# Graph layer with two mixtures of experts: the second mixture on rows sorted by expert

## The reference

```python
logits = tokens @ router_w.T
probs = softmax(logits)
rw, re = top_k(probs, 2)
rw = rw / maximum(rw.sum(-1), 1e-12)
combine = zeros((N, 8)).at[arange(N)[:, None], re].set(rw)
out = tokens                       # tokens = layernorm(x)
for e in range(8):
    h = gelu(tokens @ w1[e] + b1[e])
    y = h @ w2[e] + b2[e]
    out = out + combine[:, e:e + 1] * y
```

## Time and profile before

| | us |
|---|---|
| median of 3 runs | 2085.33 |
| lowest and highest | 2073.9, 2096.82 |
| profiled execution | 2092.29, its span 2090.3 |

### The profile page before, as it was taken

One profiled execution on the slowest core, in us unless ns is written; L12 is line 12 of the kernel. 1 busy time (PEld: TensorE's weight loads), 2 busy tenths in 40 slices (PEclk: granted clock), 3 DMA queues, 4 the chain that ended last, 5 costly groups with the idle time before them and its releaser, 6 DMA issues.

```text
span 2090.3 us, 22190 instructions
## 1 busy us (share of the span) xinstructions
PE 1752.5 (84%) x6787; PEld 1057.1 (51%) x6787; DVE 965.6 (46%) x2222; ACT 576.9 (28%) x1334; POOL 659.5 (32%) x650
## 2 busy tenths in 40 slices
PE   3899477999999899971287999999998999998875
PEld 1455123444544445541244666666666666666654
DVE  5432152133233333342377566566756666664221
ACT  2111002223122231310122434343333434343231
POOL 0000475475444540004246333233433323310000
PEclk9999688999999999985567899899998989999887
DMA  7233885364453542016567545354545444421000
GB/s 226 96 126 141 279 224 140 101 189 124 133 151 101 177 115 73 16 55 238 181 175 208 145 131 145 113 160 123 149 127 143 124 132 137 129 77 32 17 5 8
DMA packets 181022, 269.96 MB, mean 129 GB/s; under 512 B 24513, under 2 KB 140181, under 8 KB 178325
## 3 DMA queue, kind: packets, MB, share of 16 engines
q1 hardware_dynamic: 140693, 144.84, 22.1%
q0 software_dynamic: 40192, 123.51, 21.1%
HBM read 196.20 MB, written 72.06 MB: 128 GB/s over the span
## 4 chain that ended last, share of the span: by engine, by line
PE 38%; DVE 6%; ACT 3%; SPq 2%; issue 2%; DMA 2%; DVEq 0%
PE att_psR L2195 8%; PE att_psR L2222 7%; PE att_psG L2089 7%; PE att_psR L2171 4%; PE att_psR L2180 3%; PE att_psE L2070 2%; DMA att_eft<-in_eft 2%; PE att_psG L2088 1%; PE att_psQ L2063 1%; SPq L2267 1%; PE att_psR L2158 1%; PE att_psR L2135 1%; DVE att_stat L1853 1%; PE att_psR L2214 1%; PE att_psG L2086 1%
## 5 line engine op out<-in xcount | busy, mean ns | idle before, releaser
L1716 POOL DMA_INDIRECT att_kv<-table_kv,g_srcI x314 | 335.2, 1067 | 735.3 <-PE att_psG L2089 477.8
L1058 POOL DMA_INDIRECT ex_hg<-table_h,z_idx x314 | 309.0, 984 | 243.7 <-PE ex_psG L1346 162.4
L2195 PE MATMUL att_psR<-att_t,g_mw 128*128 128x256 f32 x640 | 185.7, 441 | 18.6 <-ACT att_t L2041 18.6
L1346 PE MATMUL ex_psG<-ex_hg,ex_oh 128*42 128x256 f32 x628 | 179.3, 407 | 21.5 <-DMA ex_hg<-table_h,z_idx 13.2
L2089 PE MATMUL att_psG<-att_kv,att_oh 128*42 128x264 f32 x628 | 194.5, 438 | 1.6 <-DVE att_kv L1818 1.6
L1731 DVE TENSOR_TENSOR att_kv<-att_kv,att_epb 128x1024 f32<-128x1024 f32 x79 | 96.3, 1220 | 150.0 <-ACT att_epb L1999 146.7
L2195 PEld LDWEIGHTS att_psR<-att_t,g_mw 128*128 128x128 f32 x640 | 135.8, 219 | 50.5 <-issue 29.7
L2222 PE MATMUL att_psR<-g_mw,att_h 128*128 128x256 f32 x640 | 153.5, 389 | 0.0
L702 PE MATMUL tab_psH<-e_u,tab_xT 128*128 128x512 f32 x320 | 145.2, 606 | 9.1 <-DVE e_u L506 9.1
L1944 DVE SCALAR_TENSOR_TENSOR att_acc<-att_psR,att_gate,att_acc 128x256 f32<-128x256 f32 x160 | 69.9, 478 | 152.2 <-PE att_psR L2222 152.2
L2222 PEld LDWEIGHTS att_psR<-g_mw,att_h 128*128 128x128 f32 x640 | 125.8, 197 | 22.0 <-issue 3.3
(11 more groups left out here) (305 smaller groups left out, 2456.5 us busy)
## 6 DMA issues: line engine op xcount, KB each, us to landing
table_h<-tab_hs SPq DMA_DIRECT2D x20, 1024.0 KB, 3.9
att_eft<-in_eft SPq DMA_DIRECT2D x79, 128.0 KB
ex_db<-table_dst SPq DMA_DIRECT2D x79, 126.0 KB
table_ohT<-ex_ohT SPq DMA_DIRECT2D x79, 126.0 KB
att_ohT<-table_ohT SPq DMA_DIRECT2D x79, 126.0 KB
table_oh<-ex_oh SPq DMA_DIRECT2D x79, 84.0 KB
att_oh<-table_oh SPq DMA_DIRECT2D x79, 84.0 KB
table_x<-e_x SPq DMA_DIRECT2D x10, 512.0 KB, 5.1
```

The costliest lines, as they stand in the source:

```text
L1058: nc.gpsimd.indirect_dma_start(hg[:, t % RING0, :], None, d.h[:, :], bass.IndirectOffsetOnAxis(ap=g.idx0[:, t:t + 1], axis=0)).then_inc(go ...
L1346: ins = nc.tensor.matmul(psG[0:WG, 0:D], oh[:, i % 3, t % TP, :], hg[:, t % RING0, :], start=(t % TP == 0), stop=last)
L1716: nc.gpsimd.indirect_dma_start(kv[:, t % (RINGC * TP), H:H + 2 * D], None, d.kv[:, :], bass.IndirectOffsetOnAxis(ap=g.srcI[:, t:t + 1], ax ...
L2195: ins = nc.tensor.matmul(out[:, c * CB:(c + 1) * CB], g.mw1[:, e, k, c * P:(c + 1) * P], t3[:, k, :], start=(k == 0), stop=(k == DK - 1))
```

## The change

The ten blocks are split into three parts, PARTS1. For each block, all up to `mix` runs as before, except that f and y are no longer interleaved, and acc (bias part, tokens and x) goes to a table in memory. When the last block of a part has its gates, `ranks` computes on VectorE for each row and each of its two experts a position in a list sorted by expert, every expert's rows starting at a multiple of 128, and te, the expert of each tile. GpSimd scatters the normed rows to a table (two indirect DMAs a token tile). Tiles of 128 sorted rows are then loaded, transposed (T), run through layer one (A1) and two (Y) with weights that SyncE loads for each tile by a value it reads from te, and stored. GpSimd fetches both results of each row (G), VectorE adds them with their factors (`add_experts`), and SyncE stores. The tables are filled with zeros in the stage before. The first experts' code is not changed. The resident weights are gone.

```diff
@@ stage_sums_experts, SyncE
                         for i in range(3):
                             keep_windows(i)
+                        sp.wait_ge(s.filled, 1)
+                        for table in d.sorted1:
+                            n = table.shape[0] // P
+                            sp.dma_start(table.rearrange("(t p) c -> p t c", p=P), zero[:, :].unsqueeze(1).to_broadcast([P, n, D])).then_inc(s.zeroed, 16)
                         sp.wait_ge(s.grp_stored, 16 * len(CH))
                         for i in range(2):
                             load_nodes(i)
@@
+PARTS1 = ((0, 1, 2, 3), (4, 5, 6), (7, 8, 9))
 SEGMENTS = (
     (("att", 0),),
     (("wo", 0),),
-    (("turnN", 0), ("f", 0), ("f", 1), ("y", 0), ("f", 2), ("y", 1)),
...
+    (("turnN", 0), ("f", 0), ("f", 1), ("f", 2), ("f", 3)),
+    (("f", 4), ("f", 5), ("f", 6), ("f", 7)),
+    (("y", 0), ("norm", 0)),
+    (("turnX", 0), ("logits", 0)),
+    (("mix", 0),))
+RATE1 = 1.5
+YG = 4
+def sorted_tiles(n, experts):
+    return 2 * n + experts - 1
@@ part_events: one step of a part's work
+            step.append(("T", p, k))
...
+            step.append(("A1", p, k - 1))
...
+            step.append(("Y", p, k - 2))
@@ stage_attention, GpSimd
+                        if what == "slotA" and RINGC <= b + 2 < NG:
+                            pool.wait_ge(s.summed, b + 2 - RINGC + 1)
+                            gather_group(b + 2)
+                        if what == "scatter":
+                            pool.wait_ge(s.pos_ready, b + 1)
+                            for j in range(2):
+                                t = e - token_tiles(b)[0]
+                                nc.gpsimd.indirect_dma_start(d.sorted1[b][:, :], bass.IndirectOffsetOnAxis(ap=pos[:, b, j, t:t + 1], axis=0),
+                                                             n3[:, e // BC % N3, e % BC, :], None).then_inc(scattered[b], 16)
+                        if what == "G":
+                            for j in range(3):
+                                pool.wait_ge(yb_free[j], 16 * len(range(j, tile_no(b, many(b)), 3)))
...
+                                if 2 * n + j >= YG:
+                                    pool.wait_ge(s.out_ready, n - YG // 2 + 1)
@@ TensorE
+                        if what == "A1":
...
+                            pe.wait_ge(s.xdT_ready, n + 1)
+                            pe.wait_ge(ws_got[n % 3], 32 * (n // 3 + 1))
+                            for o in range(DK):
+                                for k in range(DK):
+                                    ins = nc.tensor.matmul(out[:, o * P:(o + 1) * P], ws[:, n % 3, 0, k, o * P:(o + 1) * P], xdT[:, n % 2, k, :],
+                                                           start=(k == 0), stop=(k == DK - 1))
@@ SyncE
+                def load_weights(p, n):
+                    m_ = tile_no(p, n)
+                    if m_ >= 3:
+                        sp.wait_ge(s.y1_made, m_ - 2)
+                    expert = sp.value_load(te[0:1, p, n:n + 1], min_val=0, max_val=E1 - 1)
+                    for j, w in enumerate((d.mw1, d.mw2)):
+                        sp.dma_start(ws[:, m_ % 3, j, :, :], w[ds(expert, 1), :, :].rearrange("a (k p) o -> p (a k) o", p=P)).then_inc(ws_got[m_ % 3], 16)
...
-                        for w_sb, w in ((g.mw1, d.mw1), (g.mw2, d.mw2)):
-                            for e in range(E1):
-                                sp.dma_start(w_sb[:, e, :, :], w[e].rearrange("(k p) o -> p k o", p=P)).then_inc(g.weights1, 16)
...
+                        if what == "rank":
+                            sp.wait_ge(s.te_ready, b + 1)
+                            for n in range(3):
+                                load_weights(b, n)
+                        if what == "dispatched":
+                            sp.wait_ge(scattered[b], 32 * len(token_tiles(b)))
+                            for n in range(3):
+                                load_sorted(b, n)
+                        if what == "T" and e >= 1 and e + 2 < many(b):
+                            load_sorted(b, e + 2)
+                        if what == "Y":
+                            if e >= 1:
+                                keep_output(b, e - 1)
+                                if e + 2 < many(b):
+                                    load_weights(b, e + 2)
+                        if what == "returned":
+                            keep_output(b, many(b) - 1)
```

More of the change, by code:

```diff
@@ L1565, with part_events, put @@
     (("wo", 0),),
[8 rows of a table removed]
+    (("turnN", 0), ("f", 0), ("f", 1), ("f", 2), ("f", 3)),
[3 more added lines that the diff above has]
+    (("mix", 0),))
+PT1 = BC * max(len(p) for p in PARTS1)
+MT1 = 2 * PT1 + E1 - 1
+RATE1 = 1.5
+YG = 4
+AG = 6
+N3 = 6
+RANKS = 18
+def sorted_tiles(n, experts):
+    return 2 * n + experts - 1
+def part_events(p, tiles, experts):
+    first = [("rank", p, 0)]
+    scatter = [("scatter", p, t) for t in tiles]
+    n = sorted_tiles(len(tiles), experts)
+    work = []
+    for k in range(n + 2):
+        step = []
+        if k < n:
+            step.append(("T", p, k))
+        if 0 <= k - 1 < n:
+            step.append(("A1", p, k - 1))
+        if 0 <= k - 2 < n:
+            step.append(("Y", p, k - 2))
+        work.append(step)
+    last = [("G", p, t) for t in tiles]
+    out = [("sum", p, t) for t in tiles]
+    return first, scatter, work, last, out
 def order1(slots):
     start = [(NG // NC + 1) * (b + 1) + LAG + 2 if slots else 8 * b + 1 for b in range(NC)]
+    if slots:
+        start[-1] -= 1
+    plan = {}
+    def put(i, events):
+        plan.setdefault(i, []).extend(events)
+    free = 0
+    for p, blocks in enumerate(PARTS1):
+        first, scatter, work, last, out = part_events(p, range(blocks[0] * BC, (blocks[-1] + 1) * BC), E1)
+        i = max(start[blocks[-1]] + len(SEGMENTS), free)
+        tail = i >= slots - 2
+        put(i, first)
+        i += 1
+        while scatter:
+            put(i, [scatter.pop(0) for _ in range(len(scatter) if tail else min(2, len(scatter)))])
+            i += 1
+        put(i, [("dispatched", p, 0)])
+        owed = 0.0
+        while work:
+            owed += RATE1 if i < slots else 99.0
+            while work and owed >= 1.0:
+                put(i, work.pop(0))
+                owed -= 1.0
+            i += 1
+        put(i, [("returned", p, 0)])
+        pairs = last[:2]
+        for g_, s_ in zip(last[2:] + [None, None], out):
+            pairs += [s_] + ([g_] if g_ else [])
+        while pairs:
+            put(i, [pairs.pop(0) for _ in range(min(len(pairs), 4 if i < slots else 99))])
+            i += 1
+        free = i
     out = []
-    for i in range(start[-1] + len(SEGMENTS)):
+    for i in range(max(max(plan), start[-1] + len(SEGMENTS)) + 1):
         for b in range(NC):
@@ new lines, in stage_attention, with tile_no @@
+            for unit in {"att": ("turnA",), "wo": ("wo",), "turnN": ("turnN",), "f": ("f",), "turnX": ("turnX",), "logits": ("logits",),
+                         "mix": ("gateT", "bias"), "y": ("y",), "rank": ("rank",), "T": ("T",), "A1": ("A1",), "Y": ("Y",)}.get(what, ()):
+                bank[unit, b, e], turn_of = turn_of, (turn_of + 1) % 3
+                before[unit, b, e] = last.get(bank[unit, b, e])
+                last[bank[unit, b, e]] = (unit, b, e)
+        def tile_no(p, n):
+            return tile_base[p] + n
@@ L1719, in _ @@
+                guarded(pool, program)
             @block.vector
```

399 lines of the change are left out of this document (281 added, 118 removed), and 7 rows, old and new, of the table SEGMENTS.

## The result

The changed kernel takes 2193.3 us (median of 4 runs, 2189.13 to 2199.8) against 2082.2 for the kernel before: a ratio of 1.053, interval 1.046 to 1.060. Its profiled execution has a span of 2187.5 us, 97 more than before.

A forecast was written before the change was run, and what follows sets the result against it. It took TensorE to bound the attention stage, with removed expert pairs freeing its time but sorting lengthening the tail. Its terms summed to +55 us on the 2092 us profiled execution; from the 2085 median, 2140 us, range 2075 to 2205.

The forecast's parts named there:

- likeliest case: Whole kernel: the summed terms hold, giving 2140 us, own range 2110 to 2170; chance 0.50.
- step 4: Slots 53 to 69: 16 pairs leave (-68), 23 tiles come (+61), waits for weights add 15; +8 us.
- step 3: Slots 18 to 52, without tiles: 9.5 us a slot plus 9 for ranks, 342 us instead of 425; -83 us.
- steps 6 and 7: Tail: turnX of block 8 to turnX of block 9, +32 us; from there to the end, +100 us.
- 5 slots 70 to 77, 78 to turnX8: Slots 70 to 77 with ranks, sums and late gathers, -4 us; slots 78 to 85 with 12 tiles, +8 us.
- step 2: Start of attention: without the 16 expert weight loads, group 2's loads are issued 28 us earlier; -28 us.
- step 1: Ahead of the first edge-node loads: SyncE's 8.0 MB zero fill delays VectorE and the gathers; +22 us.
- half-clock rival: Tail tiles stay at 1.2 GHz, 5.0 us each (27 more); lean slots 0.5 us more (21): 2188 us; chance 0.16.
- rival of slow weights: Double slots and after the ranks: weight landings of 7.5 us beside gathers, 42 us more, 2182 us; chance 0.10.

The follow-up runs named there:

- e7: The kernel before, with its 18 feed-forward and second-expert weight loads moved behind later group loads in SyncE's queue, no sorting: 0.985 of the kernel before, 2051.2 us.
- e8: The changed kernel with weights loaded three steps ahead and the zero fill moved behind the last group of the sums: 1.008 of the kernel before, 2102.4 us.
- e5: The changed kernel itself, word for word, run again as control beside other runs on their chip: 1.054 of the kernel before, 2193.2 us.
- e10: The kernel of e1 (changed kernel, zero fill later) once more, run beside e9: 1.051 of the kernel before.
- e9: The kernel of e2 (changed kernel, weights three steps ahead) once more, on another chip: 1.027 of the kernel before, 2182.5 us.
- e1: The changed kernel with the sorted tables' zero fill moved behind the last group of the sums: 1.051 of the kernel before.
- e6: The changed kernel with 12 more identity products (2.76 us at full clock) on TensorE in each of slots 18 to 52: 1.067 of the kernel before.
- e2: The changed kernel with the first layer's weights loaded three steps ahead instead of one, in more weight buffers: 1.029 of the kernel before.
- e11: The kernel of e7 with identity products filling TensorE's idle time in the tail: 0.992 of the kernel before, on another chip than e7.

## Why the prediction came out as it did

Forecast: 2140 us, slower, 2075 to 2205. Measured: 2193.3. The sign and the range hold; the sum was +55, the trace has +97, and 2193 lies above the likeliest case's own range (2110 to 2170). The 42 us between them are step 4 (50 too little) and step 3 (20), less what steps 6 and 7 had too much (19) and some 10 of the rest: that the sum came as near as it did is in part luck. By its steps:

| step | forecast | trace of the change |
|---|---|---|
| 1 zero fill | +22 | +18 (slot 0 at 992 for 974) |
| 2 start of attention | -28 | -28 |
| 3 slots 18 to 52 | -83 | -63 |
| 4 slots 53 to 69 | +8 | +58 |
| 5 slots 70 to 77, 78 to turnX8 | -4, +8 | +2, -3 |
| 6 turnX8 to turnX9 | +32 | +25 |
| 7 turnX9 to the end | +100 | +88 |

**Steps 1 and 2** were right, by the rows they were read from. e7 shows that step 2 has nothing to do with sorting: a gain of the queue's order, which the dense kernel can have alone. Of step 1, e8 against e5 shows 20 us at slot 0, and e10 against e9 still 16 at slot 53; on the chip of e1 hardly anything of it is left there, and why stays open.

**Step 3** had the mechanism and missed the clock. Of the 9.5 us a slot, 7.3 were TensorE's work at the clock of before, but the lean slots' clock is 0.78, not 0.92. The same sums and features, 35 slots of before and of the change:

```profile
L2089 PE MATMUL att_psG<-att_kv,att_oh 128*42 128x264 f32 x285 | 84.2, 422 | 0.0
...
L2070 PE MATMUL att_psE<-g_we,att_eft 65*128 65x32 f32 x280 | 36.3, 275 | 0.0
```

```profile
L2318 PE MATMUL att_psG<-att_kv,att_oh 128*42 128x264 f32 x286 | 104.0, 500 | 0.0
L2299 PE MATMUL att_psE<-g_we,att_eft 65*128 65x32 f32 x280 | 44.2, 309 | 0.0
```

These two alone are 27.7 us longer, 0.8 a slot; 304 us for the 30 slots without ranks are 10.1 a slot. The half-clock rival had named this for the lean slots at 0.5 us a slot, and its larger part, the tail's tiles, did not come: they ran at 0.89 of the clock, 3.9 us apart, where the step said 4.0. The rival also placed its row wrongly: the 3.75 us at 1955.89 stand behind turnX of block 8 and not behind the idle time before 2027, as TensorE's timeline of the kernel before shows, though the same happened there:

```profile
1954.04 1.09 PE L2135 MATMUL att_psR<-g_ident,att_n 128*128 128x128 f32 x4 [4.10 <-DVE att_n L1864]
...
2029.08 3.39 PE L2195 MATMUL att_psR<-att_t,g_mw 128*128 128x256 f32 x8 [0.77 <-ACT att_t L2041]
```

The Trainium skill ("TensorE: Matmul & The Clock Gate", section "HAM oscillation - how this bites in real kernels") says that short bursts between waits pay the slow clock again and again. The lean slots (0.78) and e6 (0.93 with the fillers) agree with it. The tail's tiles do not bear on it in the same way: they stayed at 0.89, and most of their waits for weights were 1.1 to 1.8 us, shorter than the 4.10 us of the row at 1954.04.

**Step 4** is the step that failed, twice. "16 pairs leave (-68)" took the pair's 4.24 us of TensorE time as its price in a slot. Measured, it is 2.0 (e7 against e5): a pair was done in part in time in which TensorE would have idled or run at half clock, and so 16 of them give back 32, not 68, if the price of slots 18 to 47 holds here. e6 shows the same from the other side: 2.76 us of TensorE work cost 1.14. "Two slots (56, 64) stall about 5 us, the others 0 to 3: +15" had the right queue and the right landing (4.4 us median in these slots, for the 4 to 5 taken), but too few long waits: there were nine, of 4.7 on average, since SyncE holds the weights not only behind the sums' store but, twice, behind a block load that must land (14.0 us). Without these waits (e2, e8, e9) the stretch is 32 to 38 us shorter. 211 - 32 + 61 + 35 = 275 for 269 measured, so the tile's own price, 2.65 in the forecast, was about right: 2.4 by this, and 2.7 and 2.3 when e8 is held against e7 (233 us for 203) and e9 against e11 (225 for 204), each on one chip.

**Steps 6 and 7** were right in kind and together 19 us too long. From the gates' last product to the first T there were 24 us (forecast 27.5), from there to the last Y 73.6 (79.5), and the fetches took 20.7 from the last Y to the last sum (21.5); the tile step was right on average, its largest term was not. In the tail a landing takes 3.0 us median, for the 4.0 taken, and the median step is 3.7; four steps of 5.0 to 5.3 bring the mean to 3.9. The 29 us ahead of attention of block 9 were in step 6 as 31.5.
The Trainium skill ("DMA: Bandwidth & Descriptors", section "Anatomy of one DMA - SWDGE (gpsimd) path") has a fit by which 256 KB take 2.6 us, as an estimate. It is for transfers that GpSimd issues; of these, issued by SyncE, the least landing was the same, and the median of the whole run half a microsecond above it (3.1).

**What the chances missed.** The rival of slow weights (2182) and that of the half clock (2188) were held apart, and each came in part. The weights were late in the double slots, where the rival put them, and cost 32 to 38 us of its 42, but not by landings of 7.5 us (the largest in these slots was 6.6): they were issued late. Half clock came in the lean slots, the smaller half of its rival. No case had both.

**Why sorting loses.** By the prediction's count it takes 178 us of work from TensorE. In the slots a pair taken out returns 2.0 us and a tile put in costs 2.3 to 2.7, three tiles standing for four pairs, so that there the exchange itself is about even. Slots 18 to 77 lose 56 pairs and take in 23 tiles, with ranks, fetches and sums: with the weights in time they take 691 us in e8 and 719 in e7 on the same chip, 27 won. From slot 78 on, where 38 tiles stand for 24 pairs and a pair costs its 3.5 (from 2047.54 to 2050.99, the start of the next, in the kernel before), e8 takes 306 us and e7 227: 79 lost, for ranks, scatters and fetches stand in line with the tiles there, some 45 us (24 and 21) for the last part alone that no other work covers.

## What to carry to other kernels

Price work that is to be removed by what its slot gives back, not by its busy time: put in or take out work of that size and see what the span does. Here the ratio was 0.4 to 0.5, and in the lean slots the removal also slowed the clock for all that stayed. Read what a diff does beside its purpose: moving 6 MB of weights (4 of the experts, 2 of the feed-forward part) out of the front of a queue was worth 1.5% alone. A load whose issue stands behind a store that waits for another engine is as late as that engine; with more buffers, so that it could be issued three steps ahead, its place in the queue no longer mattered (e8).
